# First cross-attention: values as the stationary operand, probabilities moving, output produced transposed

## The reference, cut to what matters

```python
# L0 cross-attention: H=16 heads, KV=4 key/value groups of G=4 heads, HD=96
hidden = concat([context, latents], axis=1)          # 375 + 112 = 487 keys
q = latents @ Wq.T; k = hidden @ Wk.T; v = hidden @ Wv.T
scores = einsum('bkgqd,bksd->bkgqs', q, k) / sqrt(96)
attn = softmax(scores)
out = einsum('bkgqs,bksd->bkgqd', attn, v)           # per head, 112 x 96
return out @ Wo.T
# then: x = x + tanh(gate) * ...; a quantised linear layer; a second
# cross-attention; a linear layer with a low-rank part chosen per row
```

## Time and profile before

| what | value |
|---|---|
| median of 3 runs | 2263.5 us (2260.79 to 2269.38) |
| the profiled execution's own time | 2263.35 us |
| its span in the profile | 2261.4 us |
| TensorE matmuls busy | 2092.7 us, 93% |
| VectorE busy | 1023.7 us, 45% |
| ScalarE busy | 830.8 us, 37% |
| GpSimd busy | 756.7 us, 33% |
| TensorE busy in stage B, 540 to 1358 us | 775.42 of 818 us, granted clock 0.98 |

### The profile page before, as it was taken

The page is one execution under the profiler, slowest core; times in us unless marked ns, Lnnn a source line. Parts: engine busy times, 40 slices in busy tenths (PEclk is TensorE's granted clock), DMA queues, the critical chain, the costliest instruction groups (busy, mean ns, idle before and its releaser), DMA issues. The chain is left out here.

```text
span 2261.4 us, 39784 instructions
## 1 busy us (share of the span) xinstructions
PE 2092.7 (93%) x14930; PEld 1295.2 (57%) x14944; DVE 1023.7 (45%) x1872; ACT 830.8 (37%) x1640; POOL 756.7 (33%) x736
## 2 busy tenths in 40 slices
PE   7989999997999999999999987999999945999998
PEld 3446565654677676766667663444444423666665
DVE  5544444444443333434333432344334426666665
ACT  3422222222455554545545541121211125444442
POOL 0000000011355555555545550110111026666662
PEclk9989999998999999999999998999999977999999
DMA  5423333335023222222332315233233236666662
GB/s 166 150 71 82 75 84 73 83 102 132 31 62 91 76 62 59 62 59 62 79 87 60 74 50 154 66 84 84 53 72 83 74 102 204 200 195 195 198 196 66
DMA packets 331422, 224.09 MB, mean 99 GB/s; under 512 B 295152, under 2 KB 301040, under 8 KB 327072
## 3 DMA queue, kind: packets, MB, share of 16 engines
q1 hardware_dynamic: 244224, 195.36, 30.9%
q10 hardware_dynamic: 87072, 26.89, 5.0%
HBM read 170.49 MB, written 51.65 MB: 98 GB/s over the span
## 5 line engine op out<-in xcount | busy, mean ns | idle before, releaser
L844 POOL TENSOR_TENSOR b_probT<-b_exp,b_probT 128x448 f16<-128x448 f32 (+2 forms) x256 | 264.4, 1034 | 268.2 <-ACT b_probT L906 268.2
L411 POOL TENSOR_TENSOR cT<-ctx_raw,cT 128x375 f16<-128x375 f32 x256 | 219.9, 880 | 92.3 <-ACT cT L406 92.3
L903 ACT ACTIVATE b_exp<-b_s_ps 128x448 f32<-128x448 f32 (+2 forms) x256 | 139.0, 543 | 300.8 <-PE b_s_ps L1085 296.3
L655 PE MATMUL a_pr<-proj_q_p,a_yT 128*128 128x384 f16 x1344 | 232.8, 333 | 1.1 <-ACT a_yT L508 1.1
L1099 PEld LDWEIGHTS b_o_ps<-b_v,b_probT 128*112 128x112 f16 (+2 forms) x3072 | 199.7, 133 | 49.2 <-issue 19.4
L1099 PE MATMUL b_o_ps<-b_v,b_probT 128*112 128x97 f16 (+5 forms) x3072 | 201.7, 216 | 24.8 <-POOL b_probT L844 19.2
L1046 PE MATMUL b_kv_ps<-cT,wkv_p 128*128 128x375 f16 x1152 | 206.0, 331 | 9.0 <-PEq L419 9.0
L1050 PE MATMUL b_kv_ps<-wkv_p,cT 128*128 128x384 f16 (+1 forms) x1152 | 211.1, 326 | 0.0
L1085 PE MATMUL b_s_ps<-b_qT,b_kT 96*128 96x448 f16 (+5 forms) x768 | 192.1, 359 | 0.0
L655 PEld LDWEIGHTS a_pr<-proj_q_p,a_yT 128*128 128x128 f16 x1344 | 131.8, 100 | 88.6 <-issue 7.5
L974 DVE TENSOR_REDUCE b_nmax<-b_mx_ps 112x2 f16<-112x974 f32 x128 | 149.6, 1169 | 72.3 <-PE b_mx_ps L1062 71.5
(11 more groups left out here) (202 smaller groups left out, 2999.6 us busy)
## 6 DMA issues: line engine op xcount, KB each, us to landing
ctx_raw<-in_ctx_t SPq DMA_DIRECT2D x32, 1500.0 KB, 8.3
d_cn_raw<-in_ctx_nat SPq DMA_DIRECT2D x32, 512.0 KB
qk_scratch<-a_heads ACTq DMA_DIRECT2D x28, 480.0 KB, 6.5
b_qT<-qk_scratch SPq DMA_DIRECT2D x32, 336.0 KB, 4.5
o_scratch<-b_oT SPq DMA_DIRECT2D x128, 84.0 KB, 1.9
c_oT<-o_scratch SPq DMA_DIRECT2D x28, 384.0 KB, 6.0
d_cn_raw<-in_ctx_nat SPq DMA_DIRECT2D x16, 476.0 KB
x_scratch<-c_x SPq DMA_DIRECT2D x14, 512.5 KB, 5.8
```

The lines of the kernel that those rows point to most:

```text
L411: pool.tensor_tensor(cT[:, p, 1, k, 0:S], ctx_raw[:, k, :], cT[:, p, 0, k, 0:S], ALU.subtract).then_inc(split_lo, 1)
L655: last = mm(pr[:, c % 3, 0:KW], yT[:, p, a, k, :], weight(b, k, c), start=(n == 0 and k == 0), stop=(n == 2 and k == KD - 1))
L844: pool.tensor_tensor(pT[0:m, g % 2, c, 1, :], ex[0:m, i % 2, :], pT[0:m, g % 2, c, 0, :], ALU.subtract).then_inc(p_lo, 1)
L903: act.activation(ex[0:m, i % 2, :], s_ps[0:m, i % 2, 0:G * Q], ACT.Exp).then_inc(exped, 1)
```

## The change

Values become the stationary operand and transposed probabilities the moving one. The values' high part has 32 columns of ones beside the 96 value columns, so a matmul's output has 96 partitions of values and 32 partitions that all hold the sums, with the 4 x 112 queries of the group as columns. Each step's chunk is multiplied as soon as its own probabilities are there, three matmuls of 448 columns per step, and accumulated over the four chunks of a group. o_ps has two banks. pT keeps one group instead of two. The reciprocal is taken of 32 partitions x 448 columns three times, into three blocks of 32 partitions, so that it lines up with the 96 value rows. The output is already transposed: the six transposes, their copy and oT are gone, and the split output oo is stored as it is. The row transposes of the maxima have their place in unused columns of the scores' first bank, and move: that of the first half to step 11 of the batch before, that of the second half to step 1 of the batch itself.

```diff
-VW = HD + 2
-OC = G * HD // P
...
-                    vv = sb("b_v", [P, 2, 4, 2, KV, VW], F16)
+                    vv = sb("b_v", [P, 2, 4, 2, KV, P], F16)
...
-                    pT = sb("b_probT", [P, 2, 4, 2, G * Q], F16)
-                    rs = sb("b_rsum", [Q, 2, G], F32)
-                    o32 = sb("b_o32", [Q, 2, KW], F32)
-                    oo = sb("b_o", [Q, 2, 2, KW], F16)
-                    oT = sb("b_oT", [P, 2, 2 * OC * Q], F16)
+                    pT = sb("b_probT", [P, 4, 2, G * Q], F16)
+                    rs = sb("b_rsum", [HD, G * Q], F32)
+                    o32 = sb("b_o32", [HD, 2, G * Q], F32)
+                    oo = sb("b_o", [HD, 2, 2, G * Q], F16)
...
-                    o_ps = pb("b_o_ps", [P, HALF], F32)
-                    tr_ps = pb("b_tr_ps", [P, 1024], F16)
+                    o_ps = pb("b_o_ps", [P, 2, HALF], F32)
+
+                    tr_ps = s_ps[0:H // 2, 0, G * Q:G * Q + Q // 2].bitcast(F16)
...
+                    TURN_AT = 11
...
                         def store(b, g):
-                            sp.wait_ge(turn_free, out_turn(b, g) + 1)
+                            sp.wait_ge(o_lo, KV * b + g + 1)
                             for part in range(2):
-                                dst = o_s[part, g * G * HD:(g + 1) * G * HD, rows(b, Q)].rearrange("(c k) r -> k c r", k=P)
-                                src = oT[:, g % 2, part * OC * Q:(part + 1) * OC * Q].rearrange("k (c r) -> k c r", c=OC)
+                                dst = o_s[part, g * G * HD:(g + 1) * G * HD, rows(b, Q)].rearrange("(h d) r -> d h r", d=HD)
+                                src = oo[:, g % 2, part, :].rearrange("d (h r) -> d h r", h=G)
                                 sp.dma_start(dst, src).then_inc(o_stored[g % 2], 16)
...
                         def slot(j, p, b):
+                            load_row(p, b, 1)
                             if inside(b - 1, B):
-                                load_row(p, b, 1)
                                 if inside(b + 1, B):
                                     load_qk(j, 1 - p, b + 1)
...
-                                store(b - 1, 2)
...
                             store(b, 0)
+                            store(b, 1)
                             if inside(b + 1, B):
                                 load_row(1 - p, b + 1, 0)
-                            store(b, 1)
+                            store(b, 2)
...
-                            if c == 0:
-                                wait(act, pv, KV * b + g - 1)
-                            act.activation(pT[0:m, g % 2, c, 0, :], s_ps[0:m, i % 2, 0:G * Q], ACT.Exp).then_inc(exped, 1)
+                            wait(act, pv, n - 3)
+                            act.activation(pT[0:m, c, 0, :], s_ps[0:m, i % 2, 0:G * Q], ACT.Exp).then_inc(exped, 1)
...
                         def out_scaled(b, g):
                             n = KV * b + g
-                            dve.wait_ge(pv, n + 1)
-                            sums = o_ps[0:Q, 0:G * VW].rearrange("q (h d) -> q h d", h=G)
-                            dve.reciprocal(rs[:, g % 2, :].rearrange("q h -> q h ()"), sums[:, :, HD:HD + 1]).then_inc(summed, 1)
-                            dve.wait_ge(summed, n + 1)
+                            dve.wait_ge(pv, STEPS * b + 4 * g + 4)
+                            wait(dve, o_read, n)
+                            for k in range(G - 1):
+                                dve.reciprocal(rs[32 * k:32 * k + 32, :], o_ps[HD:P, g % 2, 0:G * Q]).then_inc(summed, 1)
+                            dve.wait_ge(summed, 3 * n + 3)
                             wait(dve, o_lo, n - 1)
-                            dve.tensor_tensor(o32[:, g % 2, :].rearrange("q (h d) -> q h d", h=G), sums[:, :, 0:HD],
-                                              rs[:, g % 2, :].rearrange("q h -> q h ()").to_broadcast([Q, G, HD]),
-                                              ALU.mult).then_inc(o_read, 1)
-
-                        def out_turned(j, p, b, g):
-                            dve.wait_ge(turned, out_turn(b, g) + 1)
-                            wait(dve, o_stored[g % 2], 32 * (2 * b + g // 2))
-                            dve.tensor_copy(oT[:, g % 2, :], tr_ps[:, 0:2 * OC * Q]).then_inc(turn_free, 1)
+                            dve.tensor_tensor(o32[:, g % 2, :], o_ps[0:HD, g % 2, 0:G * Q], rs[:, :], ALU.mult).then_inc(o_read, 1)
...
-                        dve.memset(vv[:, :, :, 0, :, HD:HD + 1], 1.0).then_inc(ones_ready, 1)
+                        dve.memset(vv[:, :, :, 0, :, HD:P], 1.0).then_inc(ones_ready, 1)
...
-                                if i % 4 == 3:
-                                    if i >= 7:
+                                if i % 4 == 1:
+                                    if i >= 5:
                                         out_scaled(b, i // 4 - 1)
...
+                        def attend(j, p, b, i):
+                            g, c = divmod(i, 4)
+                            n = KEYS[c][1]
...
+                            if c == 0:
+                                wait(pe, o_read, KV * b + g - 1)
+                            pe.wait_ge(p_lo, STEPS * b + i + 1)
+                            for x, (u, w) in enumerate(PASSES):
+                                e = HD if w else P
+                                last = mm(o_ps[0:e, g % 2, 0:G * Q], vv[0:n, p, c, w, g, 0:e], pT[0:n, c, u, :],
+                                          start=(c == 0 and x == 0), stop=(c == 3 and x == 2))
+                            last.then_inc(pv, 1)
...
-                            if t % 4 == 3:
-                                row_turned(0, t // 4)
+                        row_turned(0, 0)
                         scores(0, 0, 0, 0)
...
                             for i in range(STEPS):
-                                if i >= 4:
-                                    attend(j, p, b, i // 4 - 1, i % 4)
+                                if i >= 1:
+                                    attend(j, p, b, i - 1)
...
+                                if i == 1:
+                                    row_turned(b, 1)
+                                if i == TURN_AT and inside(b + 1, B):
+                                    row_turned(b + 1, 0)
```

More of the change, by code:

```diff
@@ L752, in kv_count @@
                         return 9 * b + (2 * k + 2 if k < 3 else k + 4)
[L757 to L762, removed]
                     def rows_turn(b, half):
-                        if isinstance(b, int) and b == 0:
-                            return half
-                        return 6 * (b - 1) + 3 + 2 * half
+                        return 2 * b + half
                     block = st.enter_context(nc.Block())
@@ L781, in load_v @@
                         def load_v(j, p, b):
-                            wait(sp, pv, KV * (b - 1))
+                            wait(sp, pv, STEPS * (b - 1))
                             for part in range(2):
@@ L868, in _ @@
                         run_slots(pool, slot, B)
-                        for g in (2, 3):
-                            out_low(B - 1, g)
+                        out_low(B - 1, 3)
                     @block.scalar
@@ L892, in row_read @@
                         def row_read(b, half):
-                            act.wait_ge(turned, rows_turn(b, half) + 1)
+                            if isinstance(b, int) and b == 0 and half == 0:
+                                act.wait_ge(turned, 1)
+                            else:
+                                act.wait_ge(scored, STEPS * b + (3 if half else TURN_AT + 2 - STEPS))
                             wait(act, row_loaded[half], 16 * b)
-                            act.activation(nrow[:, half, :], tr_ps[0:H // 2, 0:Q], ACT.Copy).then_inc(turn_free, 1)
+                            act.activation(nrow[:, half, :], tr_ps, ACT.Copy).then_inc(turn_free, 1)
                         def exponent(b, i):
@@ L1068, in row_turned @@
                             wait(pe, turn_free, rows_turn(b, half))
-                            pe.transpose(tr_ps[0:H // 2, 0:Q], nmax[:, half * H // 2:(half + 1) * H // 2],
+                            if not (isinstance(b, int) and b == 0 and half == 0):
+                                pe.wait_ge(exped, 2 * (STEPS * b + (1 if half else TURN_AT - STEPS)))
+                            pe.transpose(tr_ps, nmax[:, half * H // 2:(half + 1) * H // 2],
                                          ident[0:Q, 0:Q]).then_inc(turned, 1)
@@ L1087, in scores @@
                             last.then_inc(scored, 1)
-                        def attend(j, p, b, g, h):
-                            if h == 0:
-                                if g == 0:
-                                    pe.wait_ge(kv_lo, kv_count(b, 5))
-                                    pe.wait_ge(v_loaded[p], 32 * (j + 1))
-                                pe.wait_ge(p_lo, STEPS * b + 4 * g + 4)
-                                wait(pe, o_read, KV * b + g)
```

(29 more changed lines are left out.)

47 lines of the change are left out of this document (15 added, 32 removed).

## The result

The changed kernel takes 2562.8 us (median of 4 runs, 2558.1 to 2565.9) against 2266.3 us for the kernel before on the same chip: a ratio of 1.130 [1.128, 1.132], slower by 13%. The forecast was 2549 us. The profiled execution took 2558.1 us, 2556.3 of it span, at a mean granted clock of 0.925 (before: 0.969).

The account below looks back on a forecast made before the run. TensorE's stream was taken to bound stage B, with VectorE's longer scaling now stalling it. The profiled 2263.35 us plus 270 for 15 batches, 12 for the last batch and 4 for the head gave 2549 us, range 2440 to 2790.

Parts of the forecast that it names:

- The slope of the reciprocal: VectorE's scaling in stage B: each reciprocal column costs 6.0 ns beside 157 ns fixed, so 448 columns take 2.85 us.
- the bound of 9.0: Upper bound in ns per reciprocal column, from the one-column reciprocal with about 4 ns put down to PSUM.
- T: VectorE's time to scale one group of four heads, three reciprocals and a multiply: 9.0 us.
- the three rules: TensorE's stalls before top scores in steps 10, 14, 8: T − 1.58, T − 2.65, T − 7.8; 7.4, 6.4, 1.2 us.
- The slow clock: TensorE's half clock behind each batch's two long stalls: 2.9 us each, 5.8 us per batch.
- The stall-free batch: A stage B batch on TensorE if nothing else waited: 45.0 us against 47.8 before.
- the jump's cost stays: TensorE's loop jump, once per two batches, keeps its 2.85 us idle and the 2.9 us of slow clock behind it.
- Tail and head: Last batch with four scalings end to end, +12 us; stage B's start with the first row of maxima uncovered, +4 us.
- Rival 3: A reciprocal column costs 1.04 ns like every other operation's; T 2.3 us, 2236 us in all, faster; chance 0.10.
- rival 2: Cheaper reciprocal columns, 3.3 ns: one reciprocal takes 1.64 us, T 5.4 us, 2411 us in all; chance 0.06.
- Rival 4: At 6.0 ns per column the clock stays up or stalls overlap work counted as blocked: 2462 us; chance 0.09.
- Rival 1: Dearer reciprocal columns, 9.0 ns: T 13.1 us, larger stalls plus 1.7 us in step 4, 2821 us; chance 0.20.

Follow-up runs that it names:

- e8: Changed kernel with the sums copied to three SBUF blocks and one reciprocal on 96 partitions instead of three on 32; 2360.9 us (one run).
- e1: Changed kernel with its three reciprocals replaced by multiplications with a constant of the same shape, output not normalised; 2234.9 us, ratio 0.984.
- e2: Changed kernel with one 32x448 reciprocal per group instead of three, read by three multiplications of 32 partitions each; 2344.7 us, ratio 1.033.
- e6: e5 with the first half's row of maxima turned after four of the eight top scores again, as in the kernel before; 2215.9 us, ratio 0.979.
- e7: e6 with four batches per turn of TensorE's loop instead of two, other engines' loops kept; 2221.4 us, ratio 0.980.
- e9: e7 plus a bare TensorE wait for the last maximum at the end of every batch; 2218.7 us (one run).
- e5: Changed kernel with one reciprocal per group, in two 224-column halves behind two steps' maxima, three multiplications behind the third's; 2221.0 us, ratio 0.980.
- e3: Changed kernel with a fourth reciprocal of the same shape per group, into a tile that nobody reads; 2743.0 us (one run).
- e4: Changed kernel with all reciprocals kept, one per step behind that step's maximum, and the multiply in the fourth step; 2374.3 us, ratio 1.046.

## Why the prediction was right

**The slope of the reciprocal.** Worked out from 24 ns between two narrow rows as 6.0 ns per column, it is (2959 − 157)/448 = 6.25; halves give (1538 − 157)/224 = 6.17. The two widths by themselves, with the medians 2959 and 1558, give 6.25 and a fixed part of 157 ns, which had been borrowed from another operation. The range of 3.3 to 9.0 held it near its middle. The 4 ns that the bound of 9.0 puts down to PSUM had no row behind them; e8's reciprocal from SBUF takes 10 ns less than the one from PSUM. By the rule of the Trainium skill weighed there ("VectorE: DVE Perf Modes", "First, the fixed hardware budget", a repeat count of 8) a column would cost 8.3 ns as an estimate; the traces don't agree, with their 6.25.

**Stalls.** T was put at 9.0 and is 9.5. With it the three rules give 7.9, 6.9 and 1.7 us; 7.87 on average, 6.67 and 1.67 were measured. e1, e2 and e8 (T = 2.5, 4.9, 5.5) follow the first two to 0.2 us, e8 with 3.87 and 2.66. The size was off by 1.2 us per batch in all, some 18 us in the total.

**The slow clock.** Put at 2 × 2.9 us. Behind step 10's stall the way from its top scores to the attention of step 12 takes 7.76 us instead of 4.71, behind step 14's the way to the attention of step 0 takes 5.41 instead of 2.85: 3.05 + 2.56 = 5.6. That is one batch (961.18, 982.63); in the batches that alternate with it they take 6.54 and 4.70 (895.59, 915.82), 3.7 in all. Not foreseen: behind the stall of 1.67 us it fell in two batches (1014.91, where eight projections take 2.56 us instead of 1.30, and 1349.41) and not in the other twelve.

**The stall-free batch.** 45.0 us was worked out; e6 shows 45.25. A batch of after takes 66.8 us on average. Without 45.25 and the stalls' 16.2, 5.4 are left for the clock and for the edges of the idles, against 5.8; the prediction's batch had 65.8.

**The step that failed: "the jump's cost stays".** It went. Twelve batches of before, from one row of maxima to the same one twelve batches later, take 1258.95 − 666.64 = 592.3 us; without jumps they would take 12 × 47.8 = 573.6. So five jumps cost 18.7 us, 3.7 each (2.72 idle on average; over the next 6 us the clock was at 1.00 behind one, between 0.72 and 0.74 behind three and at 0.50 only behind the one that I had chosen). All of it is gone: the new loop body is not fetched again. A passage of the Trainium skill bears on it ("Runtime: NRT & Kernel Launch", "Instruction fetch mechanics"): a taken branch whose target isn't at hand makes the engine wait for a fetch. e7 and e9 agree, with the condition added that nothing has let the issue run ahead. The section speaks of a window of two pages, of 256 instructions each, and gives TensorE's memory as 2,048 instructions; e6 jumps back over some 1,030 without a fetch, which the first figure doesn't allow for TensorE and the second does. Where between 1,030 and 1,700 the limit lies no run here shows.

So the batches' +275.6 us against the forecast's 270 is a near hit, and in part luck, made of errors of both signs. Per batch the stalls are 1.2 us above the prediction, the stall-free batch 0.25 above and the clock 0.4 below, 15 × 1.05 = +15.8. The jumps are −18.7. The last batch that prepares another one takes 1593.95 − 1518.55 = 75.4 us, +8.6: its stalls are 5.26, 7.60 and 7.07 us, and VectorE's queue holds the low parts of stage C's weights (L977) there as well. Together +5.7.

**Tail and head.** +15.2 us against +12: four scalings run end to end 9.7 us apart (predicted 9.0), and stage C then waits for the last store. Head: +0.9 against +4. The 2.23 us of idle for the first row of maxima are there, but the same turn in e6 is worth only 35.34 − 32.86 = 2.5 us, and the clock that I had charged up to 2.9 us for did not fall there (behind the same idle in e5 it did).

**Rivals.** Rival 3's condition is what e1 sets, 2235 us for its 2236, partly by luck: it kept the jump's cost, which e1 doesn't have, and had batches of 45.8 us where e1's take 46.4. Its slope did not hold, nor did that of rival 2, with 1.64 us for a reciprocal that takes 2.96. Rival 4 fell: the clock does go down and the stalls overlap nothing. Rival 1's pattern, a fourth stall in step 4, is what e3 shows.

## What to carry to other kernels

- Work on an engine with slack is free only in pieces shorter than the slack of whoever stands behind it in the queue. VectorE was busy 37 of 90 us; one piece of 9.5 us in front of a maximum that frees a single buffer still cost 22 us per batch. With one reciprocal in place of three, cut into two pieces of 1.5 us, each behind a maximum, TensorE no longer waits; with all three, in pieces of 3 us, a batch still loses 9 us (e4).
- A sum that has been replicated over partitions need not be inverted once for each block: one reciprocal, read by three multiplies, alone saves 218 us (e2), the spreading alone 188 (e4), and both together turn 13% slower into 2% faster (342 us, e5).
- Before a term is carried over as unchanged, ask what in the code makes it; here the row transpose in the last step made the jump's idle visible, and it was being moved.

## What the runs showed of the hardware

- A reciprocal on VectorE costs about 6.2 ns per column and about 0.16 us besides: 2959 ns for 32x448 from PSUM, 2949 for 96x448 from SBUF, 1538 on average and 1558 as the median for 32x224. A multiplication over the same 448 columns takes 0.62 to 0.63 us.
- Idle of TensorE doesn't map onto its clock by length alone. In the 14 full batches of each run the clock went down to 1.2 GHz behind every idle of 3.32 us (e2), 3.87 (e8) and 6.7 and more (after). Behind shorter ones it did so at times, in some cases only in the middle of the work that followed: behind 2.66 us in none (e8), behind 2.26 to 2.55 in 13 (e4), behind 2.11 in 7 (e2), behind 1.67 in 2 (after). In the kernel before it fell behind 2.44, 2.62, 2.85 and 2.99 and stayed up behind 2.68; in e9 it fell behind 2.79 both times.
- A backward jump of TensorE's loop with some 1,700 or 2,060 matmuls and weight loads in its body fetches instructions again, one with 1,030 doesn't. A fetch packet starts 2.5 to 3.1 us ahead of the first matmul behind the jump; of that 0.4 us are idle where the issue had run ahead (e7), and 2.4 to 3.0 where a late wait stood right in front of the jump (before, e9).
